# GpSimd centres one group per slot instead of a pair every second slot, in the iterated LayerNorm stage

## The reference, cut to what matters

```python
def step(h, _):
    h = h + 0.01 * jnp.tanh(h)
    h = h * jax.nn.sigmoid(h)
    h = _layernorm(h, ln_w, ln_b)            # over the 128 channels
    h = jnp.einsum('bsc,dc->bsd', h, W) + b
    return (h, None)
x = x + scan(step, x, None, length=30)
```

## Time and profile before

| what | us |
|---|---|
| median of 3 runs (1263.76 to 1265.21) | 1264.63 |
| the profiled execution, its own time | 1265.02 |
| its span in the profile | 1263.0 |
| first three layers, up to the first scalings that follow each other steadily | about 563 |
| iterated stage after that | about 700 |

### The profile page before, as it was taken

One profiled execution on the slowest core, in us unless ns is written; L12 is line 12 of the kernel. 1 busy time (PEld: TensorE's weight loads), 2 busy tenths in 40 slices (PEclk: granted clock), 3 DMA queues, 4 the chain that ended last, 5 costly groups with the idle time before them and its releaser, 6 DMA issues.

```text
span 1263.0 us, 27914 instructions
## 1 busy us (share of the span) xinstructions
PE 1228.0 (97%) x9073; PEld 1094.9 (87%) x9073; DVE 1151.7 (91%) x3029; ACT 960.0 (76%) x1170; POOL 947.3 (75%) x667
## 2 busy tenths in 40 slices
PE   8899999999999999869999999999999999999998
PEld 7677777777777777659999999999999999999998
DVE  7988888888888887789999999999999999999996
ACT  2455555555555555769999999999999999999994
POOL 2455555555555555579999999999999999999996
PEclk9999999999999999979999999999999999999999
DMA  6111111111111000000000000000000000000004
GB/s 196 43 43 42 43 42 42 42 42 42 43 42 46 35 0 1 1 1 1 1 0 0 0 0 0 0 0 0 0 0 0 0 0 0 0 0 0 0 0 133
DMA packets 29812, 27.77 MB, mean 22 GB/s; under 512 B 3285, under 2 KB 21464, under 8 KB 29656
## 3 DMA queue, kind: packets, MB, share of 16 engines
q1 hardware_dynamic: 29784, 27.41, 6.9%
HBM read 23.21 MB, written 4.19 MB: 22 GB/s over the span
## 4 chain that ended last, share of the span: by engine, by line
PE 74%; DVE 13%; issue 5%; ACT 4%; POOL 3%; DVEq 0%; DMA 0%; SPq 0%; POOLq 0%; ACTq 0%
PE psum L894 28%; PE psum L946 15%; PE psum L679 4%; PE psum L681 4%; PE psum L680 4%; PE psum L850 4%; PE psum L911 3%; PE psum L701 3%; PE psum L696 3%; POOL h_ring L533 2%; DVE emb_n L1507 2%; DVE xh_mem L1295 1%; PE psum L690 1%; ACT emb_f L1054 1%; DVE u_ring L1329 1%
## 5 line engine op out<-in xcount | busy, mean ns | idle before, releaser
L533 POOL TENSOR_TENSOR h_ring<-g_pair,f_rs 128x1024 f32<-128x1024 f32 x240 | 451.9, 1904 | 31.5 <-DVE f_rs L1400 19.0
L1312 DVE BATCH_NORM_STATS2 f_stat<-g_pair 128x6 f32<-128x256 f32 x960 | 394.5, 425 | 2.4 <-ACT g_pair L1003 2.4
L946 PE MATMUL psum<-ident,h_ring 128*128 128x128 f32 (+1 forms) x1920 | 296.8, 277 | 7.8 <-POOL h_ring L533 6.8
L1329 DVE SCALAR_TENSOR_TENSOR u_ring<-t_ring,psum 128x1024 f32<-128x1024 f32 x232 | 281.9, 1215 | 8.1 <-ACT t_ring L1013 3.6
L946 PEld LDWEIGHTS psum<-ident,h_ring 128*128 128x128 f32 (+1 forms) x1920 | 247.7, 167 | 35.1 <-issue 7.1
L1017 ACT ACTIVATE y_all<-psum 128x1024 f32<-128x1024 f32 x240 | 244.0, 1017 | 17.2 <-PE psum L946 17.2
L894 PE MATMUL psum<-w_t,y_all 128*128 128x128 f32 x1920 | 254.5, 276 | 0.0
L894 PE MATMUL psum<-w1c_t,y_all 128*128 128x128 f32 x1920 | 253.8, 275 | 0.0
L1003 ACT ACTIVATE g_pair<-u_ring 128x1024 f32<-128x1024 f32 x240 | 251.7, 1049 | 0.9 <-DVE u_ring L1329 0.9
L1013 ACT ACTIVATE t_ring<-psum 128x1024 f32<-128x1024 f32 x232 | 238.1, 1026 | 15.6 <-PE psum L894 8.9
L894 PEld LDWEIGHTS psum<-w_t,y_all 128*128 128x128 f32 x1920 | 234.3, 192 | 0.0
(11 more groups left out here) (200 smaller groups left out, 2146.7 us busy)
## 6 DMA issues: line engine op xcount, KB each, us to landing
work<-in_adj_dram SPq DMA_DIRECT2D x16, 1024.0 KB, 5.5
x_tok<-in_x_dram SPq DMA_DIRECT2D x16, 256.0 KB, 5.6
out_dram<-y_all SPq DMA_DIRECT2D x7, 512.0 KB, 3.2
work<-in_L_gnn_conv_w_dram SPq DMA_DIRECT2D x1, 1088.0 KB
out_dram<-y_all SPq DMA_DIRECT2D x2, 256.0 KB, 3.6
work<-in_L_gnn_w_ih_dram SPq DMA_DIRECT2D x1, 384.0 KB
work<-in_L_gnn_w_hh_dram SPq DMA_DIRECT2D x1, 192.0 KB
work<-in_L_gnn_W_dram SPq DMA_DIRECT2D x1, 64.0 KB, 5.1
```

Source lines behind the costliest of these rows:

```text
L533: pool.tensor_tensor(tiles(h_ring[j % 4]), tiles(g_ring[j]), spread(f_rs[:, both(j), at:at + GT], GT, C), ALU.mult).then_inc(f_norm, 1)
L946: m = pe.transpose(g_ps[j % 2][0:rows, t // NT, P * (t % NT):P * (t % NT) + P], tiles(h_ring[j % 4])[:, t, 0:rows], ident[:])
L1312: ins = dve.bn_stats(f_stat[:, j, 0, 2 * q:2 * q + 2, :].rearrange("p t w -> p (t w)"), two)
L1329: dve.scalar_tensor_tensor(out=u_ring[k % 2], in0=t_ring[k % 2], scalar=STEP, in1=src, op0=ALU.mult, op1=ALU.add).then_inc(f_u, 1)
```

## The change

`centre` for pairs stays for groups 0 to 3 of the first iteration. Everywhere else `centre_one` centres half of a single group in every slot: four tiles, 128x512. The half is the same as before (`centred(j)`: tiles 0 to 3 of an even group, 4 to 7 of an odd one). The total of elements centred doesn't change. `scale` for group s now waits until `f_mean` is s-1, which is the count that the centring of that very group gives.

```diff
+            def centre_one(j, s):
+
+                pool.wait_ge(f_bn, s + 1)
+                half = slice(NT * centred(j), NT * centred(j) + NT)
+                pool.tensor_tensor(tiles(g_ring[j])[:, half, :], tiles(g_ring[j])[:, half, :],
+                                   spread(f_stat[:, j, 0, half, 1], NT, C), ALU.subtract).then_inc(f_mean, 1)
+
             def scale(i, j, s):
                 if isinstance(i, int) and i == 0 and j < BY_POWER:
                     pool.wait_ge(f_pow, j + 1)
+                    pool.wait_ge(f_mean, j // 2 + 1)
                 else:
                     pool.wait_ge(f_root, pairs(i, j) + 1)
-                pool.wait_ge(f_mean, i * (GROUPS // 2) + j // 2 + 1)
+                    pool.wait_ge(f_mean, s - 1)
                 wait(pool, f_turn, s - 3)
...
                 newer = earlier(it, k, LAG_M)
-                if newer is not None and k % 2 == 0:
-                    centre(*newer[1:])
+                if newer is not None and not (ends(it, 0) and k == EARLY):
+                    centre_one(*newer[1:])
```

## The result

The changed kernel takes 1289.51 us, median of 4 runs (1289.32 to 1289.98), against 1264.46 for the kernel before in the same comparison. The ratio is 1.0198, 95% interval 1.0185 to 1.0210: 25 us slower. The forecast was 1294, in a range of 1280 to 1311.

What follows compares the result with a forecast made beforehand. TensorE and GpSimd were taken to need equal time; GpSimd would then bound at 3.71 + 2 x (1.05 + 0.155) = 6.12 us a pair. Over 116 intervals that adds 29.1 us: 1265.0 + 29.1 = 1294.1, range 1280 to 1311.

Steps and rivals of the forecast that it cites:

- The bound: Iterated stage: GpSimd's own work takes 5.78 us for a pair of slots, the same as TensorE's to within 0.02.
- The half instruction: GpSimd's 128x512 centring: claimed 1.05 us, with 0.20 us fixed and 1.67 ns an element.
- The silence: GpSimd's gap between a centring and the scaling waiting for it: 0.155 us, twice a pair instead of once.
- The late root hidden: Loop from one even scaling through the other engines to the next root: 10.1 us, fitting within 10.36 by 0.3.
- the 10.3 us of excess: Time above GpSimd's 5.78 us a pair, 0.089 x 116, mostly waits for late roots; claimed to go under the new bound.
- The odd group's delay: Odd groups' scaling comes 1.15 us later relative to even ones, using up TensorE's 1.0 us lead; nothing waits beyond that.
- The ends of the stage: Last odd group is scaled 1.2 us later relative to the even one; cost put at nothing, within 1.2 us.
- The two-operand rule: GpSimd centring at about 2.6 cycles an element: half an estimated 1.11 us, cadence 6.24, time about 1308.
- What the profile after was to show: Halves of 1.05 us, no `f_rs` releases, GpSimd over 94% busy, pairs 6.12 us apart, TensorE waiting about 0.17 a slot.
- not below 1.08: Rival, chance 0.06: GpSimd's half 0.955 and silence 0.08, together below 1.08 us; time 1265, or 1254.7 without late roots.
- the half wasn't dearer than 1.13: Rival, chance 0.07: GpSimd's half costs above 1.13 us, time over 1312; at 1.314 it would be 1357.
- the loop stayed inside the cadence: Rival, chance 0.10: the loop through the other engines doesn't fit, root stays late by 0.09 a pair: 1304 us.

Runs made afterwards that it cites:

- no_centring: The kernel before without GpSimd's centring in the slots, all tiles using the mean-free weights (output isn't the reference's): 1260.41 us.
- half_early: The changed kernel with each half centred one slot earlier, so no scaling waits for the instruction right before it: 1262.65 us.
- two_halves_in_a_row: The kernel before with a pair's centring split into two 128x512 instructions one behind the other, the scaling waiting for the second alone: 1271.33 us.
- extra_silence: The kernel before with one unneeded wait more: each odd group's scaling waits until its even group's scaling is done: 1267.22 us.
- quarters: The changed kernel with each half centred by two 128x256 instructions one behind the other, the scaling waiting for the second alone: 1323.38 us.
- pair_early: The kernel before with a pair's single centring moved one place earlier, between the even and the odd scaling of the group before: 1306.36 us.

## Why the prediction was right

*The bound.* The step that mattered was to see, behind a busy share of 75%, that GpSimd's own work took 5.78 us for a pair where TensorE took 5.76 to 5.78. no_centring and half_early confirm it: relief of GpSimd brings 2 to 4 us, and the change, which loads it, costs 25.

*The half instruction.* 1.05 was taken, 1.045 measured, which is 1.2 us of the time. The fixed part came from a 4-element operation (0.21 us, 0.20 taken), and the runs give 0.18 to 0.19.

*The silence.* 0.155 was taken, 0.133 measured in most slots and 0.141 on average. This is the term that was mis-sized most, 3.2 us of the time. The reason given for 0.155, that the same two kinds of instruction stand on its two sides, doesn't hold: the same two have 0.078 to 0.219 between them, by the record that carries the wait. Half and silence together make the sum 6.12 where 6.082 was measured, 116 x 0.038 = 4.4 us of the 4.5 between forecast and result. With the measured values the sum comes out: 3.71 + 2 x (1.045 + 0.141) = 6.082.

*The late root hidden.* Right. From the third pair on, the root is written at least 0.45 us before the scaling that needs it, 0.22 more than the usual 0.235 of the kernel before, where the prediction had a margin of 0.3. And the 10.3 us of excess that the kernel before had are inside the new bound. This is also why each part alone costs less than its share: two_halves_in_a_row lengthens the queue by 0.14 a pair and the real cadence by 0.060, extra_silence by up to 0.13 and 0.025. Together they cost 0.213. The first 0.08 us or so are covered by waits that were there already; what comes after it is paid in full, as quarters shows: 0.295 a pair, 34.2 us by 116 intervals, and 33.9 measured.

*The odd group's delay.* "Nothing waits beyond that" was right in this kernel. pair_early shows that the same argument has an end: between 3.03 and 3.72 us behind the even group it costs 42 us against the kernel before, with nothing else made longer.

*The ends of the stage* were put at nothing within 1.2 us; the span less the intervals differs by 25.0 - 24.7 = 0.3.

*The two-operand rule* of the Trainium skill (GPSIMD Engine Reference, 3.1 Elementwise), about 2.6 cycles an element, isn't what these centrings show: 1.68 ns an element is 2.0 cycles at that page's 1.2 GHz, and the half measured 1.045 us, where the rule gave an estimated 1.11. What the Trainium skill (GPSIMD Engine Reference, 2.1 Instruction dispatch) says, that each instruction is dispatched by a software routine, fits with a part of 0.18 to 0.19 us that doesn't depend on the size. The same section of the Trainium skill asks for a wait on the producer's semaphore where an instruction reads partitions that another of the engine's cores wrote. Here the centring and the scaling work on the same partitions, and no run leaves the wait between them out, so what that would save, and whether the result would stay right, is open.

*What the profile after was to show.* The 1.05 us, the missing `f_rs`, GpSimd's 95% and the even cadence were there. Waits of TensorE for `h_ring` of 0.17 in nearly all slots weren't to be seen as such: TensorE is some 0.15 us later in each slot, but only its starts show it, and the list of waits has no such row in this stretch.

*The rivals.* Half and silence together took 1.19 us, not below 1.08, the half wasn't dearer than 1.13, and the loop stayed inside the cadence. The first one's other part, a silence of 0.08, does occur, but at two of 16 slots.

## What to carry to other kernels

Where several engines share one cadence, write down for each the sum of its starts over one period, silences and lost overlaps included, and price a change against the smallest slack; busy shares and the chain that ended last named TensorE here, when GpSimd set the pace. Splitting an instruction on GpSimd cost 0.14 to 0.15 us of its queue each time here, and a consumer right behind its producer on the same engine cost the overlap of 0.04 to 0.05 us and a silence as well; moving the producer one place ahead (half_early) took both back and 27 us with them. Before moving it, check what then stands between two results that another engine wants evenly: the same step with the whole pair in one instruction cost 42 us.

## What wasn't expected of the hardware

- The silence between an instruction and the one that waits for it on GpSimd takes values from 0.078 to 0.219 us, the same one each time at the same slot of the loop body. It goes with the record that carries the wait: 0.078 where the waiting instruction carries it itself, 0.133 to 0.219 where a record in front does (0.143 and 0.169 with the other order of the waits). The order changes which slot has which, and the mean hardly (0.141 and 0.139).
- GpSimd's tensor_tensor with one mean repeated along a tile is linear over 256, 512 and 1024 elements: 0.617, 1.045 and 1.910 us.
- The waits of TensorE of some 0.15 us a slot don't show as idle time. They go into a later start under a record that still runs (0.96 in place of 0.89 us after the products) and a longer record (0.68 in place of 0.61 us for four transposes), while the engine counts as busy for 705.50 of 705.51 us.
